# Cross-attention and a mixture of experts on one core: blocks turned two ahead, a table in pieces, result rows and stores moved

## The reference

```python
x = x + xattn(layernorm(x), ctx_1024, mask, Wq, bq, Wk, bk, Wv, bv)
skip = layernorm(x)
xn = rms_norm(skip, norm_scale)
scores_topk, idx = top_k(xn @ w_router.T, 2)
weights = softmax(scores_topk)
up = moe_linear(xn twice, idx, w_up)       # row i gets W[idx[i]], 512 columns
u, gate = split(up, 2)
down = moe_linear(u * silu(gate), idx, w_down)
x = x + (sum(down * weights) + skip)
```

## Time and profile before

| | |
|---|---|
| median of 3 runs | 446.13 us (444.86 to 447.12) |
| the profiled execution, its time | 445.29 us |
| its span | 443.5 us |
| PE busy | 372.8 us, 84% of the span |
| DVE busy | 321.6 us, 73% |
| ACT busy | 275.5 us, 62% |
| POOL busy | 237.8 us, 54% |

### The profile page before, as it was taken

One profiled execution on the slowest core, in us unless ns is written; L12 is line 12 of the kernel. 1 busy time (PEld: TensorE's weight loads), 2 busy tenths in 40 slices (PEclk: granted clock), 3 DMA queues, 4 the chain that ended last, 5 costly groups with the idle time before them and its releaser, 6 DMA issues. The chain is left out here.

```text
span 443.5 us, 9911 instructions
## 1 busy us (share of the span) xinstructions
PE 372.8 (84%) x2608; PEld 341.4 (77%) x2608; DVE 321.6 (73%) x1349; ACT 275.5 (62%) x646; POOL 237.8 (54%) x377
## 2 busy tenths in 40 slices
PE   2559988999998999899899989978895999999850
PEld 1359888888898988888888989866674888888640
DVE  2466777877877886887788778976678677777582
ACT  1146666666767666676666776664674787787540
POOL 1062232565565565656656655543777766666460
PEclk9969999999999999999999999999999999999985
DMA  4943633725727628438347266040222453334828
GB/s 156 294 130 128 235 115 157 239 81 223 231 63 260 188 83 286 144 122 287 88 177 261 76 217 171 13 98 13 61 76 77 115 130 91 91 86 136 287 67 260
DMA packets 57526, 66.65 MB, mean 150 GB/s; under 512 B 5856, under 2 KB 49136, under 8 KB 57472
## 3 DMA queue, kind: packets, MB, share of 16 engines
q1 hardware_dynamic: 53120, 56.99, 40.7%
q0 software_dynamic: 4320, 8.92, 6.0%
q10 hardware_dynamic: 32, 0.10, 0.1%
HBM read 53.88 MB, written 12.11 MB: 149 GB/s over the span
## 5 line engine op out<-in xcount | busy, mean ns | idle before, releaser
L1307 PE MATMUL ps<-attention,ctx_sb 128*128 128x128 f32 (+1 forms) x832 | 114.2, 279 | 15.2 <-ACT attention L724 8.9
L1307 PEld LDWEIGHTS ps<-attention,ctx_sb 128*128 128x128 f32 (+1 forms) x832 | 102.5, 191 | 20.3 <-issue 10.4
L641 POOL DMA_INDIRECT parts<-mbias,blk_x x71 | 69.9, 984 | 35.1 <-ACT mbias L794 26.7
L574 POOL DMA_INDIRECT rows_in<-kept,place x64 | 68.9, 1077 | 20.4 <-issue 10.8
L724 ACT ACTIVATE attention<-ps 128x512 f32<-128x512 f32 x96 | 55.2, 594 | 35.0 <-PE ps L1289 35.0
L541 POOL TENSOR_TENSOR rstd<-ve,minus_half 128x2 f32<-128x2 f32 x32 | 25.0, 781 | 75.8 <-DVE ve L930 75.8
L871 DVE CUSTOM_DVE_ANT_0 attention<-ps,mbias 128x1608 f32<-128x1608 f32 x32 | 58.6, 1832 | 7.3 <-issue 7.3
L1289 PE MATMUL ps<-ident,attention 128*128 128x128 f32 (+1 forms) x416 | 61.0, 273 | 0.0
L701 ACT ACTIVATE attention<-attention,ebias 128x1601 f32<-128x1601 f32 x32 | 52.1, 1629 | 10.2 <-DVE ebias L889 10.0
L1273 PE MATMUL ps<-ctxt_high,gt_high 128*128 128x402 f32 x128 | 48.7, 381 | 9.6 <-DVE wr_sb L1105 6.2
L1216 DVE SCALAR_TENSOR_TENSOR mbias<-mbias,ps 128x256 f32<-128x256 f32 x71 | 29.9, 421 | 29.0 <-ACT mbias L781 29.0
(11 more groups left out here) (149 smaller groups left out, 812.7 us busy)
## 6 DMA issues: line engine op xcount, KB each, us to landing
ctxt_in<-ctx_cols SPq DMA_DIRECT2D x16, 800.5 KB, 6.3
mbias<-mbias_dram SPq DMA_DIRECT2D x16, 800.5 KB, 5.1
ctx_sb<-ctx_rows SPq DMA_DIRECT2D x16, 768.0 KB
blk_x<-rows_in SPq DMA_DIRECT2D x71, 65.0 KB, 1.9
attention<-parts SPq DMA_DIRECT2D x8, 512.0 KB, 5.8
x_in<-x SPq DMA_DIRECT2D x16, 128.0 KB, 4.4
wup_in<-w_up_t SPq DMA_DIRECT2D x8, 256.0 KB, 4.8
out<-base_all SPq DMA_DIRECT2D x8, 256.0 KB, 5.5
```

Of the source, the lines that this page charges most:

```text
L574: pool.indirect_dma_start(rows_in, bass.IndirectOffsetOnAxis(ap=place[:, c, u:u + 1], axis=0), kept[:, u % KEPT, c], None).then_inc(s_scat ...
L641: pool.indirect_dma_start(parts, bass.IndirectOffsetOnAxis(ap=blk_x[:, m % XR, D:D + 1].bitcast(I32), axis=0), blk_y[:, m % YR], None).the ...
L1307: last = pe.matmul(ps_o[:, 0:P], ctx_sb[0:n, j, t], probs_t[0:n, t * P:(t + 1) * P], start=t == 0, stop=t == KT - 1)
```

## The change

Four things. (1) Blocks are turned two ahead: xt_high and xt_low get three copies, and in a step the turn of block m + 2 stands behind the up products of block m, where the turn of block m + 1 stood at the step's start. ACT's copy of it stands behind tanh, DVE's split behind h. The PSUM bank of the turn stays one. (2) The second table is made in pieces, one or two operations in each of the steps 15 to 28 but two (TABLE_STEP is LAST_RANK + 3), instead of in three lumps; the row ends get a semaphore of their own (s_ends). The late slots stand after steps 0, 2, 6 and 9, and the last ranking in step 12. (3) SP loads all block rows, then all result rows. (4) ACT stores groups 0 to 5 after its last step; SP stores groups 6 and 7.

```diff
-    LATE_SLOTS = [0, 2, 5, 8]
-    LAST_RANK = 11
+    LATE_SLOTS = [0, 2, 6, 9]
+    LAST_RANK = 12
+    TABLE_STEP = LAST_RANK + 3
+    AHEAD = 2
...
-        xt_high = sb("xt_high", [P, 2, P], F32R)
-        xt_low = sb("xt_low", [P, 2, P], F32R)
+        xt_high = sb("xt_high", [P, AHEAD + 1, P], F32R)
+        xt_low = sb("xt_low", [P, AHEAD + 1, P], F32R)
...
+        def store(eng, n):
+
+            eng.wait_ge(s_final, n + 1)
...
             for m in range(NB):
                 load_block(m)
                 if FILL_LOAD <= m < FILL_LOAD + E:
                     fill_end(m - FILL_LOAD)
-                n = m - PART_LOAD
-                if 0 <= n < FIRST_UNITS // CH:
-                    load_parts(CH * n, CH)
-            for n in range(STORED_EARLY):
-                store(n)
-            for u in range(FIRST_UNITS, UNITS, CH):
+            for u in range(0, UNITS, CH):
                 load_parts(u, CH)
-            for n in range(STORED_EARLY, UNITS // CH):
-                store(n)
+            for n in range(FIRST_UNITS // CH, UNITS // CH):
+                store(sp, n)
...
             def step(m):
-                if is_block(m + 1):
-                    block_xt(m + 1)
                 if is_block(m):
...
                     act.activation(th[:, m % 2], ps[:, 2 + m % 2, H:H2], ACT.Tanh, scale=0.5).then_inc(s_th, 1)
+                if is_block(m + AHEAD):
+                    block_xt(m + AHEAD)
...
-            run(act, slot, lambda: block_xt(0), step)
+            run(act, slot, before_steps, step)
+
+            for n in range(FIRST_UNITS // CH):
+                store(act, n)
...
+            def table_rest(n):
+
+                js = NB - FULL
+                passed = past[:, 0:js * SEGMENTS].rearrange("p (j s) -> p j s", s=SEGMENTS)
+                if n == 0:
+                    dve.tensor_copy(row_end[:], ends_f[:, 1]).then_inc(s_ends, 1)
+                    then(dve.tensor_tensor(filled[:], ends_f[:, 1].unsqueeze(2).broadcast_to([P, E, UNITS]), limit[:], ALU.is_gt))
+                if n == 1:
+                    then(dve.tensor_reduce(reached[:, 2], filled[:], AX.X, ALU.add))
...
+                if n == 5:
+                    then(dve.tensor_tensor(passed, begins[:, 1:SEGMENTS + 1].unsqueeze(1).broadcast_to([P, js, SEGMENTS]),
+                                           count_f[:, FULL:NB].unsqueeze(2).broadcast_to([P, js, SEGMENTS]), ALU.is_le))
+                if n == 7:
+                    then(dve.tensor_reduce(owner_f[:, 0:js], passed, AX.X, ALU.add))
...
             def step(m):
-                if is_block(m + 1):
-                    split_block(m + 1)
                 if is_block(m):
...
+                if is_block(m + AHEAD):
+                    split_block(m + AHEAD)
                 if m == LAST_RANK + 1:
                     find_places(B - 1)
-                if m == LAST_RANK + 3:
-                    table_all()
-                if m == LAST_RANK + 5:
-                    table_owners(FULL, NB, SEGMENTS)
-                if m == LAST_RANK + 6:
-                    table_starts(FULL, NB, SEGMENTS)
+                table_rest(m - TABLE_STEP)
...
-                if is_block(m + 1):
-                    turn_block(m + 1)
                 if is_block(m):
...
                     last.then_inc(s_up, 1)
...
+                if is_block(m + AHEAD):
+                    turn_block(m + AHEAD)
                 if is_block(m - 2):
```

More of the change, by code:

```diff
@@ L457, in load_block @@
                     scattered(UNITS)
+                if m == FULL:
+                    sp.wait_ge(s_owner, PHASES)
                 if k == 0 or m == FULL:
@@ L768, in block_xt, with before_steps @@
                 act.wait_ge(s_bxt, m + 1)
-                wait(act, s_up, m - 1)
-                act.activation(xt_high[:, m % 2], ps[:, 0, 0:P], ACT.Copy).then_inc(s_xt_high, 1)
+                wait(act, s_up, m - AHEAD)
+                act.activation(xt_high[:, m % (AHEAD + 1)], ps[:, 0, 0:P], ACT.Copy).then_inc(s_xt_high, 1)
+            def before_steps():
+                for m in range(AHEAD):
+                    block_xt(m)
             def step(m):
-                if is_block(m + 1):
-                    block_xt(m + 1)
                 if is_block(m):
@@ L1154, in table_full, with table_rows @@
                 order_segments(E)
[L1156 to L1170, removed]
+            def table_rows():
+                passed = past[:, 0:FULL * E].rearrange("p (j s) -> p j s", s=E)
+                then(dve.tensor_tensor(passed, begins[:, 1:E + 1].unsqueeze(1).broadcast_to([P, FULL, E]),
+                                       count_f[:, 0:FULL].unsqueeze(2).broadcast_to([P, FULL, E]), ALU.is_le))
+                then(dve.tensor_reduce(owner_f[:], passed, AX.X, ALU.add))
+                dve.tensor_scalar(owner[:, 0:FULL], owner_f[:], E - 1.0, None, ALU.min)
+                then(dve.tensor_tensor(passed, passed, jump[:, 0:E].unsqueeze(1).broadcast_to([P, FULL, E]), ALU.mult))
+                then(dve.tensor_reduce(start_f[:], passed, AX.X, ALU.add))
+                dve.scalar_tensor_tensor(start_row[:, 0:FULL], count_f[:, 0:FULL], float(P), start_f[:], ALU.mult,
+                                         ALU.add).then_inc(s_owner, 1)
@@ L1173, in table_owners @@
                                                   ALU.add))
[L1174 to L1187, removed]
+                if n == 9:
+                    dve.tensor_scalar(owner[:, FULL:NB], owner_f[:, 0:js], E - 1.0, None, ALU.min)
+                if n == 10:
+                    then(dve.tensor_tensor(passed, passed, jump[:].unsqueeze(1).broadcast_to([P, js, SEGMENTS]), ALU.mult))
+                if n == 12:
+                    then(dve.tensor_reduce(start_f[:, 0:js], passed, AX.X, ALU.add))
+                if n == 13:
+                    dve.scalar_tensor_tensor(start_row[:, FULL:NB], count_f[:, FULL:NB], float(P), start_f[:, 0:js], ALU.mult,
+                                             ALU.add).then_inc(s_owner, 1)
             def split_block(m):
                 dve.wait_ge(s_xt_high, m + 1)
-                wait(dve, s_up, m - 1)
-                dve.tensor_tensor(xt_low[:, m % 2], ps[:, 0, 0:P], xt_high[:, m % 2].bitcast(F32),
+                wait(dve, s_up, m - AHEAD)
+                dve.tensor_tensor(xt_low[:, m % (AHEAD + 1)], ps[:, 0, 0:P], xt_high[:, m % (AHEAD + 1)].bitcast(F32),
                                   ALU.subtract).then_inc(s_xt_low, 1)
@@ L1233, in step, with before_steps @@
                     (sum_choices, add_base)[n // 2 % 2](n // 4)
-            run(dve, slot, lambda: split_block(0), step)
+            def before_steps():
+                for m in range(AHEAD):
+                    split_block(m)
+            run(dve, slot, before_steps, step)
             for n in range(SUMMED_EARLY, 2 * (UNITS // CH)):
@@ L1460, in before_steps @@
                 load_owners(0)
-                turn_block(0)
+                for m in range(AHEAD):
+                    turn_block(m)
             run(pe, slot, before_steps, step)
```

28 lines of the change are left out of this document (17 added, 11 removed).

## The result

| | before | after |
|---|---|---|
| median | 446.62 us (444.86 to 448.94) | 454.65 us (453.96 to 455.19) |
| profiled execution; its span | 445.29; 443.5 us | 454.58; 452.5 us |

The ratio of the medians is 1.0176 (95% interval 1.0126 to 1.0226): the change makes the kernel slower by 8.0 us. The forecast was 451.8, with 0.66 on slower.

A forecast was written before the change was run, and what follows sets the result against it. PE was taken to bound the blocks' middle, with waits at their start and end. Terms 15.3 - 6.9 + 0.6 + 0.9 - 3.8 - 0.4 = +5.7 on 445.29 gave 451.0, as a median 451.8 us; range 444 to 456.5.

The forecast's parts named there:

- loop, 61 steps: Blocks 9 to 70: each turn waits for DVE's split, 0.25 us a step, +15.3 us (9.8 to 18.3).
- tables: Second table on DVE: pieces instead of lumps win 6.9 us; four large pieces cost 0.6 (0 to 1.2).
- late slots: Up to block 9: attention slots moved later, with ACT's work behind a waiting high copy, +0.9 us (0 to 2).
- result rows behind block rows: Blocks 64 to 70: with block rows loaded first, PE's waits for them go, -3.8 us.
- tail: Loads, sums and stores behind the last blocks: earlier stores from ACT, -0.4 us (-1 to +0.8).
- The order on PE decides: PE's queue in each block step: the turn, asked for earlier with one bank, must wait; array's cost 0.16 us a step.
- The rival in which the loop does not bind: Block steps: the split comes before the turn's new place, steps stay near 1.5 us, 438 to 438.5 us; chance 0.10.
- PE idle once a step ahead of the turn: Sign for blocks 20 to 64: PE idles each step until DVE's split releases it, pace 1.7 to 1.8 us.
- The sequencer comes on top: PE's sequencer behind a waiting turn: 0.09 to 0.14 us a step beyond the array's cost.
- So it isn't waited for: Sum in step 66: the first part of the result rows lands in time at 1.75 us a step.
- at 1.5 us a step it would be late by up to 0.5: Sum in step 66: at the faster pace the first part of the result rows comes up to 0.5 us late.
- the collision: Tail: ACT's stores delay the two last loads, 0.8 us at most; full collision with loop cost 0.30 gives 457 us.

The follow-up runs named there:

- 1: Changed kernel with PE's turn and ACT's high copy of block m + 2 moved to the end of the step: 440.54 us, ratio to before 0.9871.
- 4: Changed kernel, order kept, with turned rows alternating between two PSUM banks from block 19 on: 442.52 us, ratio to before 0.9887.
- 2: Kernel before with two blocks ahead alone (three copies, turn behind the up products): 460.22 us, ratio 1.0309.
- 5: Kernel before with the second table in pieces, late slots and last ranking as changed, all else as before: 447.23 us, ratio 1.0017.
- 6: Kernel before with the table in pieces, the change's late slots and 16 instead of 12 buffers of block rows: 446.59 us, ratio 1.0005.
- 7: Changed kernel with one block ahead, turn at the step's start; tables, late slots, result rows and stores as changed: 444.45 us, ratio to before 0.9951.
- 11: Kernel before with 16 instead of 12 buffers of block rows, nothing else: 446.23 us, ratio 0.9992.
- 9: Changed kernel with the turn at the step's end and 16 instead of 12 buffers of block rows: 438.58 us, ratio to before 0.982.
- kernel 8: Kernel before with result rows loaded behind all block rows and six groups stored by ACT, nothing else: 444.32 us, ratio 0.9941.
- 3: Changed kernel with expert 0 for every block and no register loaded on PE: 448.64 us, a single execution.
- 10: Changed kernel with two PSUM banks for the turned rows and 16 buffers of block rows: 437.58 us, ratio to before 0.980.

## Why the prediction was right, by its own steps

The side, the place and the size of the main term held; three small terms were off, and one was missing. The forecast's +5.7 falls 3.3 short of the 9.0 between the spans, and the missing term (1.7) and the late slots (1.5) make almost all of that. The terms:

| term | predicted | measured | how |
|---|---|---|---|
| loop, 61 steps | +15.3 | +15.6 | 61 x (1.763 - 1.507) |
| tables | -6.3 | -6.4 | 9 to 20: -4.0 less 2.8 of the loop; +0.4 left in 20 to 64 |
| late block rows, block 23 | not seen | +1.7 | 3.50 - 1.76 |
| late slots | +0.9 | +2.4 | 0 to 9 |
| up to block 0 | 0 | +0.4 | 296.04 - 295.69 |
| result rows behind block rows | -3.8 | -3.5 | 64 to 70: -2.0 less 1.5 of the loop |
| tail | -0.4 | -1.2 | 18.86 - 20.05 |

The loop's term stands on the forecast's base of 1.507; on the 1.501 of blocks 45 to 63 it is 16.0, and what is left for the others falls by 0.4. The terms of the tables and of the result rows are not measured by themselves: they are what their stretches leave behind the loop. The +0.4 up to block 0 is within the scatter of that stretch, 294.65 to 296.21 in the thirteen profiled kernels.

- **The order on PE decides: right.** 20 to 64 took 79.70 where 72.5 or more was the mark. From the up products' end, 401.00, to the next waiting weight load, 402.64, are 1.64, the 1.64 of the forecast. Two kernels that take away only the wait, one by order (1), one by a bank (4), come back to 1.511 and 1.472; a kernel with nothing but the turn's new place (2) has 1.761. The rival in which the loop does not bind is what 1 and 4 are: 440.5 and 442.5, and with the rows no longer late 437.6, where it stood at 438. One sign was put wrongly: PE idle once a step ahead of the turn. Its own rows show that at every second turn between 362 and 387 us, and elsewhere the weight loads' rows have to be read.
- **The sequencer comes on top: right.** The step costs 0.26 more (0.25 taken), and 0.18 with a fixed expert; so the array's share is 0.18 where I had 0.16, and the sequencer's 0.08 where I had 0.09 to 0.14. The Trainium skill (TensorE: Matmul & The Clock Gate, the table of specifications) has PE's queue pull weight loads ahead of matmuls in flight. The traces agree for a turn that is free to go (weight load at 401.41, turn at 401.64, in 4) and show that it does not reach past a wait: in the changed kernel the waiting turn's load and product start at 400.86 and 400.89, and the next weight load, that of the hidden's turn, only behind them.
- **The tables: right as a sum, wrong in why.** I credited the pieces; 5, 6 and 7 show that pieces of this size are free only behind a split that is itself a block early. Alone they give nothing. Parts (1) and (2) need each other, and the price of (1) was hidden in its place in the queue.
- **The late slots: a term that was mis-sized**, +0.9 for +2.4. The loop term began at block 9; the same wait in the nine steps before, 0.26 each, would make 2.3, and 2 shows +2.4 with the slots unmoved. That is an argument and not shown: 5, 6 and 7 have +1.3 with the slots moved and no turn that waits early, and between kernels that differ up to block 9 in nothing but the row buffers, or in nothing at all, this stretch differs by up to 1.6 (24.95 before and 26.56 in 11; 26.11 in 1 and 27.52 in 9; 27.40 in the changed kernel and 28.66 in 4).
- **Late block rows: missing**, +1.7. I asked what is late next behind the table and looked at DVE alone. POOL was the one: its four late scatters and its sends, 1.26 us apart, set when a row buffer is free.
- **The result rows: right in the gain, short in the wait.** "So it isn't waited for" is 0.62 on DVE in the changed kernel, which costs PE little; "at 1.5 us a step it would be late by up to 0.5" is 1.54 in kernel 8, three times as much, and then the gain in the blocks is gone (12.62).
- **The tail: the end better than thought, the collision elsewhere.** The final stores take 2.55 behind the last addition instead of 3.0 to 3.4. ACT's stores were issued from 437.72 on, beside the last send rather than beside the two loads: it landed in 3.04 instead of 2.30. The loads in turn gained: from the landed send to the last addition's end are 6.60 instead of 7.26. The likely reason is that before SP's queue issued seven stores right behind the loads. Timelines of the changed kernel (the first two rows) and of before:

```profile
437.72 5.25 ACTq L382 DMA_DIRECT2D out<-base_all  x6
443.50 0.81 SPq L488 DMA_DIRECT2D attention<-parts  x2
...
433.43 6.67 SPq L483 DMA_DIRECT2D out<-base_all  x7
```

The Trainium skill's rule (Trainium Kernel Development and Optimization, Key Constraints) that DMAs of all issuing engines share the 16 DMA engines has this trace with it: a second queue moved the contention and did not remove it.

## What to carry to other kernels

Before an instruction is moved ahead in an engine's queue, ask how early the result it waits for is there; if its buffer is single, "earlier" can mean only that it waits in front of others; here a second buffer or a later place in the queue was the cure. A change in several parts can hide the loss of one behind the gain of another: here the parts that gained needed the one that lost, in a better place. When a bottleneck stage is shortened, look at every ring of buffers that ran under it, and at the queue of the engine that frees them.

## What the hardware showed that I had not expected

- With a wait shortly ahead of them, matmuls whose addresses come from registers cost 0.08 us a step (1.763 against 1.679 with fixed addresses, four of them 0.71 against 0.61). Where nothing waits, in 4, the same four take 0.61 with their registers.
- The last send (an indirect DMA of POOL) landed in 2.29 to 2.31 us in the five kernels in which SP stores, before, 2, 5, 6 and 11, and in 2.92 to 3.22 in those in which ACT's stores run at the time, the changed one, 1, 3, 4, 7, 8, 9 and 10. The latter are also the kernels with the result rows behind all block rows; the two were not separated.
- POOL's indirect DMAs follow one another at 1.26 us, 0.95 of it busy; with 128 rows each, this is 0.25 us short of PE's step of 1.51, so a burst of four scatters would take some twenty steps to be made up for (4 x 1.26 / 0.25, an estimate).
